# Who copies the second half of the turned probabilities out of PSUM: ScalarE before, VectorE after

## The chip, the cores and the metric

The kernel runs on one core of one Trainium2 chip. The time is the device time of one execution in microseconds; of the kernel before, three runs took 2648.97, 2649.49 and 2653.16 us, median 2649.49.

## The reference, cut to what matters

The input `x` is 128 sequences of 64 tokens with 256 features. The network has two blocks: a transformer block with modulation (attention and MLP), and a second block with attention over 16 heads of 64 features, with normalised queries and keys, followed by eight experts that each pick their tokens. The change lies in the attention of the second block:

```
h = _ln(x, ln1_g, ln1_b) + shift
qkv = (h @ Wqkv.T).reshape(b, n, 3, H, HD)
q = _ln(qkv[:, :, 0].transpose(0, 2, 1, 3), qn_g, qn_b)
k = _ln(qkv[:, :, 1].transpose(0, 2, 1, 3), kn_g, kn_b)
v = qkv[:, :, 2].transpose(0, 2, 1, 3)
scores = jnp.einsum('bhnd,bhmd->bhnm', q, k) / jnp.sqrt(jnp.float32(HD))
attn = jax.nn.softmax(scores, axis=-1)
o = jnp.einsum('bhnm,bhmd->bhnd', attn, v)
x = x + o.transpose(0, 2, 1, 3).reshape(b, n, H * HD) @ Wout.T
```

## The kernel before, in words

The phases run one after the other with a barrier between them: setup, first attention, MLP, second attention (`attention1_phase`, lines 847 to 1196), routing, experts. In the second attention a step `i` handles one tile of 128 tokens, which is two sequences of 64. There are NT = 64 tiles. Each engine has its own instruction stream, written out by hand, with semaphores between the streams; a step of any stream holds work for several tiles at once: `has(0)` guards the work on tile `i` (queries, keys, values), `has(-1)` that on tile `i-1` (softmax, product with the values, output projection), `has(-2)` the end of tile `i-2` (residual, gate scores, store) and `has(1)` the layer norm of tile `i+1`. An engine takes its instructions strictly in the order of its stream, so a wait holds up all that stands behind it.

The part of a step in which the change lies, stream by stream:

- TensorE (from line 1086): scores of tile `i-1` (L1097), products for queries and keys (lines 115 to 117 through `split_product`) and values, gate scores (L1147), the probabilities of tile `i-1` turned in two groups of four transposes, the first into `b_b[0]`, the second into `b_b[1]` (L1157, semaphores `pT0` and `pT1`), `turn_qk(0, 1)` (four transposes, L1111), the wait for the copied probabilities (L1164), the product of probabilities and values (L1173, 64 small matmuls), `turn_qk(1, QG)` (12 transposes, each group of four behind `qkn`), and the output projection, whose first half waits for the first `o_lo` and whose second half waits for the second. `turn_next` (L1118) turns `xhat` of the next tile between the halves.
- ScalarE (from line 903): squares of queries and keys (L919) with the exponentials (L906) after the first, `values_out(0)` (L911), gate scores (L929), the two copies of the turned probabilities from PSUM into `PT` (L934), `values_out(1)`, the high parts `o_hi` (L941), `qT` and `kT` (L944, L946).
- VectorE (from line 972): `hT`, `h_hi`, `h_lo` (L997 to L1007), residual, row maximum and shift of the scores, sums and moments of the squares (L975, L991), sum and scale of the probabilities (L1045 to L1053), `sums(2)`, `moments(2)`, `scaled(0)`, `sums(3)`, `moments(3)`, then `xhat` (L1066), `scaled(1)`, `scaled(2)`, `scaled(3)` (L983, query and key groups read from PSUM and multiplied by the inverse root), and the two `o_lo` (L1075).
- GpSimd: the inverse roots (L961, L966), one per group, each behind its `moments`.

Two PSUM tensors of one bank each, `b_b[0]` and `b_b[1]`, serve in turn the transposed probabilities, the output of L1173, the projection and the turned `xhat`.

Of the kernel before, what the change touches and what calls it, by code (L numbers as in the profile page):

```python
# [90 lines left out]
def pipeline_by(by, eng, step, n, before, after):  # L91


    def edge(i):
        step(i, lambda k: 0 <= i + k < n, i % by)
    first = after + -after % by
    last = n - before - (n - before - first) % by
    for i in range(-before, first):
        edge(i)
    with eng.Fori(0, (last - first) // by) as turn:  # L100
        for phase in range(by):
            step(by * turn + first + phase, lambda k: True, phase)
    for i in range(last, n + after):
        edge(i)


def later(t):

    return not isinstance(t, int) or t > 0
# [737 lines left out]
def attention1_phase(nc, a, out, g):  # L847

    with ExitStack() as ctx:
# [19 lines left out]
        PT = m.sb("a1_PT", [P, H // 2, P])  # L869
        o_hi, o_lo = (m.sb("a1_o_" + n, [P, V1], F32R) for n in ("hi", "lo"))  # L870
        xs = m.sb("a1_xs", [P, D])
        xsT = m.sb("a1_xsT", [P, DC, P])
# [3 lines left out]
        BK = 512  # L876
        b_b = [m.ps(f"a1_bb{n}", BK) for n in range(2)]
        names = ("stats aggr eps rstd xhat xT hT h_hi h_lo qk sq red vq rq qkn qkT q_out k_out v v_out s maxed "
                 "shifted exped summed recip probs pT0 pT1 pT_out o o_hi o_lo proj res xsT xsT_out lg lg_out "
                 "stored wout wv_in wv_hi wv_lo wout_hi wout_lo pe_held").split()  # L880
        s = {n: m.sem("a1_" + n) for n in names}
        ident = g.cst[:, C_ID:C_ID + P]
# [5 lines left out]
        with nc.Block() as block:  # L888
            @block.sync
            def _(sp):  # L890
                def store(t):
                    sp.wait_ge(s["res"], t + 1)
                    sp.dma_start(g.tok_dram[t][:, 0:D], xs[:, :]).then_inc(s["stored"], 16)
                    sp.dma_start(out[t], xs[:, :]).then_inc(s["stored"], 16)
                sp.dma_start(wv, a["qkv1_w"][:, :, QK1:]).then_inc(s["wv_in"], 16)
                sp.dma_start(wout[:, :, :], a["out1_w"]).then_inc(s["wout"], 16)
                with sp.Fori(0, NT) as t:
                    store(t)
                sp.wait_ge(s["stored"], 32 * NT)

            @block.scalar
            def _(act):
                def step(i, has, turn):
                    def exps():
                        act.wait_ge(s["shifted"], i)
                        nc.scalar.activation(pr[:, :, :], pr[:, :, :], ACT.Exp, scale=SCALE1).then_inc(s["exped"], 1)  # L906

                    def values_out(n):
                        act.wait_ge(s["v"], 2 * i + n + 1)
                        for b in range(2):  # L910
                            nc.scalar.copy(vs[n * S:(n + 1) * S, turn % 2, b, :],  # L911
                                           b_a[b * S:(b + 1) * S, n * BK:(n + 1) * BK]).then_inc(s["v_out"], 1)

                    if has(0):
                        for n in range(QG):
                            act.wait_ge(s["qk"], QG * i + n + 1)
                            if later(i):
                                act.wait_ge(s["red"], QG * i + n - QG + 1)
                            nc.scalar.activation(sq[:, n * BK:(n + 1) * BK], b_qk[:, n * BK:(n + 1) * BK],  # L919
                                                 ACT.Square).then_inc(s["sq"], 1)  # L920
                            if n == 0 and has(-1):
                                exps()
                    elif has(-1):
                        exps()
                    if has(0):
                        values_out(0)
                    if has(-2):
                        act.wait_ge(s["lg"], i - 1)
                        nc.scalar.copy(g.lg[:, :, bass.ds(i - 2, 1)], b_b[1][:, 0:E].unsqueeze(2))\  # L929
                            .then_inc(s["lg_out"], 1)  # L930
                    if has(-1):
                        for n in range(2):
                            act.wait_ge(s[f"pT{n}"], i)
                            nc.scalar.copy(PT[:, 4 * n:4 * n + 4, :].rearrange("p j q -> p (j q)"), b_b[n][:, :])\  # L934
                                .then_inc(s["pT_out"], 1)
                    if has(0):
                        values_out(1)
                    if has(-1):
                        act.wait_ge(s["o"], i)
                        for n in range(2):  # L940
                            nc.scalar.copy(o_hi[:, n * BK:(n + 1) * BK], b_b[n][:, :]).then_inc(s["o_hi"], 1)  # L941
                    if has(0):
                        act.wait_ge(s["qkT"], i + 1)
                        nc.scalar.activation(qT[:, :, :].rearrange("p j t -> p (j t)"), b_qk[:, 0:V1], ACT.Identity,  # L944
                                             bias=g.qn[:, 1:2], scale=g.qn[:, 0:1]).then_inc(s["q_out"], 1)
                        nc.scalar.activation(kT[:, :, :].rearrange("p j t -> p (j t)"), b_qk[:, V1:QK1], ACT.Identity,  # L946
                                             bias=g.kn[:, 1:2], scale=g.kn[:, 0:1]).then_inc(s["k_out"], 1)
                    if has(0) and not later(i):
                        act.wait_ge(s["wout"], 16)
                        nc.scalar.copy(wout_hi, wout[:, :, :]).then_inc(s["wout_hi"], 1)  # L950
                act.wait_ge(s["wv_in"], 16)
                nc.scalar.copy(g.wv_hi, wv).then_inc(s["wv_hi"], 1)
                act.wait_ge(g.loaded1, 16 * 3)
                pipeline_by(2, act, step, NT, 0, 3)

            @block.gpsimd
# [14 lines left out]
            def _(dve):  # L971
                def step(i, has):
                    def sums(n):
                        dve.wait_ge(s["sq"], QG * i + n + 1)
                        nc.vector.reduce_sum(ss[:, n * 8:(n + 1) * 8],  # L975
                                             sq[:, n * BK:(n + 1) * BK].rearrange("p (h d) -> p h d", d=HD1), AX)\
                            .then_inc(s["red"], 1)
# [11 lines left out]
                    def moments(n):  # L989
                        dve.wait_ge(s["red"], QG * i + n + 1)  # L990
                        nc.vector.tensor_scalar(vq[:, 8 * n:8 * n + 8], ss[:, 8 * n:8 * n + 8], 1.0 / HD1, EPS1,  # L991
                                                ALU.mult, ALU.add).then_inc(s["vq"], 1)
# [63 lines left out]
                    if has(0):  # L1056
                        sums(2)
                        moments(2)
                        scaled(0)
                        sums(3)  # L1060
                        moments(3)
                    if has(1):
                        dve.wait_ge(s["rstd"], i + 2)
                        if later(i + 1):
                            dve.wait_ge(s["xT"], i + 1)
                        nc.vector.tensor_scalar(xhat[:, :], g.X[:, i + 1, :], mv[:, 0:1], rstd[:, 0:1],  # L1066
                                                ALU.subtract, ALU.mult).then_inc(s["xhat"], 1)
# [17 lines left out]
            def _(pe):  # L1085
                def step(i, has, turn):
# [63 lines left out]
                    if has(-1):  # L1150
                        pe.wait_ge(s["probs"], i)
                        for n in range(2):
                            if n == 1 and has(-2):
                                pe.wait_ge(s["lg_out"], i - 1)
                            for k in range(4):
                                j = 4 * n + k
# [4 lines left out]
                    if has(0):  # L1161
                        turn_qk(0, 1)
                    if has(-1):
                        pe.wait_ge(s["pT_out"], 2 * i)  # L1164
                        pe.sem_inc(s["pe_held"], 1)
                        for mm in range(4):
                            for b in range(2):
                                toks = slice(b * S, (b + 1) * S)
                                for c in range(2):
                                    for r in range(2):  # L1170
                                        keys = slice(r * S, (r + 1) * S)
                                        j = 2 * mm + c
                                        last = nc.tensor.matmul(  # L1173
                                            b_b[r][c * HD1:(c + 1) * HD1, mm * P + b * S:mm * P + (b + 1) * S],
                                            vs[keys, (turn - 1) % 2, b, j * HD1:(j + 1) * HD1], PT[keys, j, toks],
                                            start=True, stop=True)
                        last.then_inc(s["o"], 1)
# [704 lines left out]
```

## Time and profile before

| | |
|---|---|
| median of three runs | 2649.49 us |
| profiled execution, device time | 2653.02 us |
| its span, first to last instruction | 2651.1 us |
| mean granted TensorE clock over the span | 0.958 |
| PE busy over the span | 2433.6 us (92%) |
| PE weight loads busy | 2108.6 us (80%) |
| DVE (VectorE) busy | 1966.7 us (74%) |
| ACT (ScalarE) busy | 1527.5 us (58%) |
| POOL (GpSimd) busy | 1037.3 us (39%) |

The names in the profile are PE for TensorE's matmuls and transposes, PEld for its weight loads, DVE for VectorE, ACT for ScalarE and POOL for GpSimd. A busy time is the sum of an engine's instruction times; consecutive instructions of one engine may overlap a little. L12 is line 12 of the kernel before; where a helper issues the matmul (lines 115 to 117) the tile names tell which product it is. The second attention lies between about 985 and 2130 us of the span.

### The profile page before, as it was taken

The page shows a single profiled execution, that of the slowest core. Times are in us where ns is not written, and L with a number is a line of the kernel's source. Part 1 is how long each engine was busy: PE and PEld are TensorE (multiplying, and loading weights), DVE is VectorE, ACT ScalarE, POOL GpSimd, SP SyncE. Part 2 cuts the span into 40 slices and gives each one's busy share as a digit, 9 for nine tenths or more (in the row PEclk, how much of TensorE's full clock was granted, in tenths as well). Part 3 has the DMA queues.
Part 4 walks back from the last instruction along what each step waited for, and adds up shares of the span by engine and source line. Part 5 has one row for each costly group of instructions (what it writes and reads, how often), then busy time and mean ns, then how long its engine had stood idle before and what let it go on. Part 6 is the DMA issues. An engine that isn't in the chain of part 4 may idle for free. (4 is left out here: it accounts for less than half of the span.)

```text
span 2651.1 us, 68410 instructions
## 1 busy us (share of the span) xinstructions
PE 2433.6 (92%) x25692; PEld 2108.6 (80%) x25692; DVE 1966.7 (74%) x3788; ACT 1527.5 (58%) x2847; POOL 1037.3 (39%) x876
## 2 busy tenths in 40 slices
PE   5999999969999989999999999999999824999997
PEld 4777777749999968888888888888888713899996
DVE  4888888856666658888888888888888768666663
ACT  2777777746666645555555655565556503555653
POOL 1676777730000013344333443344334302355544
PEclk8999999969999989999999999999999956999998
DMA  4011111010110110000000000000000021243332
GB/s 121 30 32 36 32 32 36 28 25 23 30 30 20 29 50 13 16 12 16 16 16 13 14 16 16 16 12 16 16 16 12 17 56 41 80 91 91 78 71 32
DMA packets 86352, 89.19 MB, mean 34 GB/s; under 512 B 26753, under 2 KB 80641, under 8 KB 83585
## 3 DMA queue, kind: packets, MB, share of 16 engines
q1 hardware_dynamic: 73984, 71.08, 8.9%
q0 software_dynamic: 12288, 17.05, 4.0%
q8 instruction: 51, 0.84, 0.1%
q14 instruction: 29, 0.23, 0.0%
HBM read 62.40 MB, written 25.69 MB: 33 GB/s over the span
## 5 line engine op out<-in xcount | busy, mean ns | idle before, releaser
L966 POOL TENSOR_TENSOR a_rq<-a_vq,minus_half 128x8 f32<-128x8 f32 x256 | 417.3, 1651 | 104.2 <-DVE a_vq L991 104.2
L919 ACT ACTIVATE a_sq<-a_bqk 128x512 f32<-128x512 f32 x256 | 152.0, 594 | 318.1 <-PE a_bqk L117 318.1
L961 POOL TENSOR_TENSOR a_rstd<-a_veps,minus_half 128x1 f32<-128x1 f32 x64 | 35.3, 552 | 628.4 <-DVE a_veps L1035 628.4
L115 PE MATMUL a_bqk<-wqk_hi,a_h_lo 128*128 128x512 f32 x512 | 207.3, 405 | 5.1 <-DVE a_h_lo L1007 5.1
L117 PE MATMUL a_bqk<-wqk_hi,a_h_hi 128*128 128x512 f32 x512 | 201.7, 394 | 0.0
L116 PE MATMUL a_bqk<-wqk_lo,a_h_hi 128*128 128x512 f32 x512 | 201.3, 393 | 0.0
L983 DVE TENSOR_TENSOR a_qk<-a_bqk,a_rq 128x512 f32<-128x512 f32 x256 | 170.6, 687 | 28.8 <-POOL a_rq L966 28.8
L1663 DVE TENSOR_TENSOR e_u_lo<-e_u,e_u_hi 128x512 fp32r<-128x512 f32 x128 | 88.8, 693 | 127.3 <-ACT e_u_hi L1526 123.2
L431 POOL TENSOR_TENSOR a_kbd<-a_kT,consts_sb 128x512 f32<-128x512 f32 x128 | 130.9, 1044 | 125.7 <-PE a_bs L556 122.5
L911 ACT COPY a_vs<-a_ba 64x512 f32<-64x512 f32 x256 | 149.0, 582 | 53.6 <-PE a_ba L117 48.9
L1521 ACT ACTIVATE e_u<-e_bu,e_b 128x512 f32<-128x512 f32 x128 | 88.3, 690 | 156.6 <-PE e_bu L117 152.7
L975 DVE TENSOR_REDUCE a_ss<-a_sq 128x8 f32<-128x512 f32 x256 | 173.2, 677 | 1.4 <-ACT a_sq L919 1.4
L680 ACT ACTIVATE m_u<-m_bu,m_b 128x512 f32<-128x512 f32 x128 | 88.4, 691 | 130.2 <-PE m_bu L117 130.2
L115 PE MATMUL a_bb<-w_parts,a_o_lo 128*128 128x256 f32 x512 | 155.9, 304 | 1.5 <-DVE a_o_lo L1075 1.4
L773 DVE TENSOR_TENSOR m_u_lo<-m_u,m_u_hi 128x512 fp32r<-128x512 f32 x128 | 88.3, 690 | 91.5 <-ACT m_u_hi L687 89.4
L698 POOL TENSOR_TENSOR m_rstd<-m_veps,minus_half 128x4 f32<-128x4 f32 x16 | 21.7, 1355 | 322.4 <-DVE m_veps L714 322.4
L123 PE MATMUL e_by<-e_w_hi,e_u_lo 128*128 128x256 f32 x512 | 145.4, 284 | 0.0
L123 PE MATMUL m_by<-w_parts,m_u_lo 128*128 128x256 f32 x512 | 145.2, 284 | 0.0
L125 PE MATMUL e_by<-e_w_hi,e_u_hi 128*128 128x256 f32 x512 | 144.8, 283 | 0.0
L124 PE MATMUL e_by<-e_w_lo,e_u_hi 128*128 128x256 f32 x512 | 144.8, 283 | 0.0
L116 PE MATMUL a_bb<-w_parts,a_o_hi 128*128 128x256 f32 x512 | 143.9, 281 | 0.0
L117 PE MATMUL a_bb<-w_parts,a_o_hi 128*128 128x256 f32 x512 | 143.8, 281 | 0.0
(244 smaller groups left out, 7828.6 us busy)
## 6 DMA issues: line engine op xcount, KB each, us to landing
X<-in_x SPq DMA_DIRECT2D x64, 128.0 KB
a_gate<-gates_of_rows SPq DMA_DIRECT2D x128, 64.0 KB, 2.5
m_gate<-gates_of_rows SPq DMA_DIRECT2D x32, 256.0 KB, 4.3
tokens<-a_xs SPq DMA_DIRECT2D x64, 128.0 KB, 1.7
out<-a_xs SPq DMA_DIRECT2D x64, 128.0 KB, 1.7
e_w<-in_fc1s SPq DMA_DIRECT2D x8, 1024.0 KB, 4.7
e_w<-in_fc2s SPq DMA_DIRECT2D x8, 1024.0 KB, 4.8
a_w<-in_fc_w SPq DMA_DIRECT2D x2, 1024.0 KB, 6.2
```

The lines of the kernel that those rows point to most:

```text
L115: tensor.matmul(to, w_lo, x_hi, start=start, stop=False)
L116: tensor.matmul(to, w_hi, x_lo, start=False, stop=False)
L117: return tensor.matmul(to, w_hi, x_hi, start=False, stop=stop)
L123: tensor.matmul(to, w_lo, x_hi, start=start, stop=False, skip_group_check=True)
L124: tensor.matmul(to, w_hi, x_lo, start=False, stop=False, skip_group_check=True)
L125: return tensor.matmul(to, w_hi, x_hi, start=False, stop=stop, skip_group_check=True)
L431: last = nc.gpsimd.tensor_tensor(kbd[:, c, :, :], kT[:, c, :].unsqueeze(1).to_broadcast([P, 4, P]), g.cst[:, C_QUAD:C_QUAD + 4].unsqueeze( ...
L911: nc.scalar.copy(vs[n * S:(n + 1) * S, turn % 2, b, :], b_a[b * S:(b + 1) * S, n * BK:(n + 1) * BK]).then_inc(s["v_out"], 1)
L919: nc.scalar.activation(sq[:, n * BK:(n + 1) * BK], b_qk[:, n * BK:(n + 1) * BK], ACT.Square).then_inc(s["sq"], 1)
L966: nc.gpsimd.tensor_tensor(rq[:, 8 * n:8 * n + 8], vq[:, 8 * n:8 * n + 8], g.mhalf[:, 0:8], ALU.pow).then_inc(s["rq"], 1)
L975: nc.vector.reduce_sum(ss[:, n * 8:(n + 1) * 8], sq[:, n * BK:(n + 1) * BK].rearrange("p (h d) -> p h d", d=HD1), AX)\
L983: nc.vector.tensor_tensor(qk[:, n * BK:(n + 1) * BK].rearrange("p (h d) -> p h d", d=HD1), b_qk[:, n * BK:(n + 1) * BK].rearrange("p (h d) ...
```

## The change

ScalarE's loop over both halves becomes a copy of the first half alone. VectorE gets the second half, between `moments(3)` and `xhat`, behind a wait for `pT1`, and counts it in a semaphore of its own. TensorE waits for both counts. The data, the buffers and the order of everything else stay.

```diff
@@ scalar
                     if has(-1):
-                        for n in range(2):
-                            act.wait_ge(s[f"pT{n}"], i)
-                            nc.scalar.copy(PT[:, 4 * n:4 * n + 4, :].rearrange("p j q -> p (j q)"), b_b[n][:, :])\
-                                .then_inc(s["pT_out"], 1)
+                        act.wait_ge(s["pT0"], i)
+                        nc.scalar.copy(PT[:, 0:4, :].rearrange("p j q -> p (j q)"), b_b[0][:, :])\
+                            .then_inc(s["pT_out"], 1)
@@ vector
                         scaled(0)
                         sums(3)
                         moments(3)
+                    if has(-1):
+                        dve.wait_ge(s["pT1"], i)
+                        nc.vector.tensor_copy(PT[:, 4:8, :].rearrange("p j q -> p (j q)"), b_b[1][:, :])\
+                            .then_inc(s["pT_out_v"], 1)
                     if has(1):
                         dve.wait_ge(s["rstd"], i + 2)
@@ tensor
                     if has(-1):
-                        pe.wait_ge(s["pT_out"], 2 * i)
+                        pe.wait_ge(s["pT_out"], i)
+                        pe.wait_ge(s["pT_out_v"], i)
                         pe.sem_inc(s["pe_held"], 1)
```

## Rows read from the trace of the kernel before

**Rows 1.** Stretches of one step each (start:end, length, busy time and count per engine).
```profile
core 0: us, PE busy (x) PEld busy (x) DVE busy (x) ACT busy (x) POOL busy (x), PEclk, DMA share, GB/s
1500.00:1517.64 17.64, 17.31 (x222) 15.12 (x221) 14.66 (x30) 10.33 (x17) 7.08 (x5) 1.00 0.04 15
...
sum 141.12, PE 138.48 PEld 120.84 DVE 117.39 ACT 82.70 POOL 56.60; mean PE 17.31 PEld 15.11 DVE 14.67 ACT 10.34 POOL 7.07
```

**Rows 2.** Waits from 1008 to 2110 us (total us, times, longest).
```profile
DVE a_hT L997 <- PE a_bb L1118: 91.6, 62, 1.5
...
DVE a_o_lo L1075 <- ACT a_o_hi L941: 30.4, 62, 0.6
DVE a_qk L983 <- POOL a_rq L966: 27.6, 63, 0.8
...
PE a_bb L1173 <- ACT a_PT L934: 20.9, 63, 0.4
...
PEld a_bb L115 <- DVE a_o_lo L1075: 12.4, 62, 0.2
...
DVE a_xs L1014 <- issue: 7.4, 41, 0.2
```

**Rows 3.** Instructions of one step in order of time (start, length, idle before).
```profile
1518.80 1.16 PE L1157 MATMUL a_bb<-consts_sb,a_p 128*128 128x128 f32 x8
...
1519.25 0.17 DVE L991 TENSOR_SCALAR a_vq<-a_ss 128x8 f32<-128x8 f32 x1
1519.33 0.41 DVE L1066 TENSOR_SCALAR a_xhat<-X,a_mv,a_rstd 128x256 f32 x1
1519.47 1.11 ACT L934 COPY a_PT<-a_bb 128x512 f32<-128x512 f32 x2 [0.23 <-PE a_bb L1157]
1519.66 1.28 DVE L983 TENSOR_TENSOR a_qk<-a_bqk,a_rq 128x512 f32<-128x512 f32 x2
...
1520.69 1.05 PEld L1173 LDWEIGHTS a_bb<-a_PT,a_vs 64*64 64x64 f32 x64 [0.54 <-issue]
1520.72 1.16 PE L1173 MATMUL a_bb<-a_PT,a_vs 64*64 64x64 f32 x64 [0.33 <-ACT a_PT L934]
1521.38 0.69 DVE L983 TENSOR_TENSOR a_qk<-a_bqk,a_rq 128x512 f32<-128x512 f32 x1 [0.43 <-POOL a_rq L966]
...
1521.81 1.53 PE L1111 MATMUL a_bqk<-consts_sb,a_qk 128*128 128x128 f32 x12
1521.94 1.08 ACT L941 CAST a_o_hi<-a_bb 128x512 fp32r<-128x512 f32 x2 [0.15 <-PE a_bb L1173]
1522.56 1.29 DVE L1075 TENSOR_TENSOR a_o_lo<-a_bb,a_o_hi 128x512 fp32r<-128x512 f32 x2 [0.49 <-ACT a_o_hi L941]
1523.30 0.19 PEld L115 LDWEIGHTS a_bb<-w_parts,a_o_lo 128*128 128x128 f32 x1 [0.20 <-DVE a_o_lo L1075]
...
1523.38 1.21 ACT L944 ACTIVATE a_qT<-a_bqk,qn 128x1024 f32<-128x1024 f32 x1 [0.37 <-PE a_bqk L1111]
...
1524.49 1.20 ACT L946 ACTIVATE a_kT<-a_bqk,kn 128x1024 f32<-128x1024 f32 x1
...
1524.77 0.38 PE L1118 MATMUL a_bb<-consts_sb,a_xhat 128*128 128x128 f32 x2
...
1525.31 0.61 DVE L997 SCALAR_TENSOR_TENSOR a_hT<-a_bb,ln1g,shift 128x128 f32<-128x128 f32 x2 [1.46 <-PE a_bb L1118]
...
1526.28 0.42 DVE L1007 TENSOR_TENSOR a_h_lo<-a_hT,a_h_hi 128x256 fp32r<-128x256 f32 x1
...
1526.46 1.16 PE L1097 MATMUL a_ba<-a_kT,a_qT 64*64 64x64 f32 x64
```

**Rows 4.** All instructions of line 934 (min/median/max ns, first and last start).
```profile
L934 ACT COPY a_PT<-a_bb x128: 586/586/591, 1008.2 to 2117.6; 128x512 f32<-128x512 f32 x128
```

**Rows 5.** Groups from 1026 to 2096 us (busy us, mean ns, idle before).
```profile
L934 ACT COPY a_PT<-a_bb 128x512 f32<-128x512 f32 x122 | 67.0, 586 | 14.4 <-PE a_bb L1157 14.4
...
L1041 DVE COPY a_xsT<-a_bb 128x256 f32<-128x256 f32 x61 | 25.5, 418 | 0.0
...
L1005 DVE CAST a_h_hi<-a_hT 128x256 fp32r<-128x256 f32 x61 | 18.0, 294 | 2.1
```

More of the change, by code:

```diff
@@ L878, in attention1_phase @@
         names = ("stats aggr eps rstd xhat xT hT h_hi h_lo qk sq red vq rq qkn qkT q_out k_out v v_out s maxed "
-                 "shifted exped summed recip probs pT0 pT1 pT_out o o_hi o_lo proj res xsT xsT_out lg lg_out "
+                 "shifted exped summed recip probs pT0 pT1 pT_out pT_out_v o o_hi o_lo proj res xsT xsT_out lg lg_out "
                  "stored wout wv_in wv_hi wv_lo wout_hi wout_lo pe_held").split()
```

## The prediction

> **What bounds the kernel now.** I read the page first for the three engines' shares, then the stretches of the second attention, then its waits, then one step in order of time. The change touches only that phase. Its loop makes 64 steps; ScalarE's first copy of the turned probabilities starts at 1008.2 us and its last at 2117.6 [rows 4], which over 63 intervals is 17.61 us a step. TensorE's matmuls cover 17.31 us of a 17.64 us step at a granted clock of 1.00, VectorE's work 14.67 and ScalarE's 10.34 [rows 1]. So TensorE's order sets the period: a step gets longer by what TensorE is made to stand in it, and by nothing else. It stands twice now. It waits for ScalarE's copies before the product with the values (PE L1173, 20.9 us in 63 steps, 0.33 each), and for VectorE's low part before the output projection (the weight load of L115 behind `o_lo`, 12.4 us in 62, 0.20 each) [rows 2]. Between these two waits lies everything that the change moves.
>
> In one step [rows 3] the reader should see this. The eight transposes of the probabilities run from 1518.80 to 1519.96. ScalarE copies both halves back to back, 1519.47 to 1520.58, so the second half is copied while VectorE is already further on: at 1519.42 it has finished `moments(3)` (L991), and it goes straight on to `xhat` (1519.33, started before the former had drained), `scaled(1)` and `scaled(2)` (1519.66), waits 0.43 for GpSimd's root, does `scaled(3)` (1521.38), waits 0.49 for ScalarE's `o_hi` and starts `o_lo` at 1522.56. TensorE loads its first value tile at 1520.69, 0.11 behind the copy's end, and the first projection weight at 1523.30, 0.05 behind the end of the first `o_lo` (1522.56 + 0.69).
>
> **The change, part by part.** *Removed from ScalarE*: one 128x512 copy of 0.586 us a step [rows 5]. What follows it there is `values_out(1)`, then the wait for `o`. The values are wanted only by the next step's products and `o_hi` waits for TensorE, so ScalarE's saved time is worth nothing: it already stands for 0.15 us before `o_hi` [rows 3].
>
> *Added to VectorE*: a wait for the second four transposes and a copy, placed ahead of `xhat` and `scaled(1..3)`. The wait is real. Those transposes end at 1519.96; VectorE is free at 1519.42. It restarts 0.16 behind a transpose (L1118 ends at 1524.77 + 0.38 = 1525.15, L997 starts at 1525.31) [rows 3], so the copy starts at 1520.12 and the engine loses 0.70 us. For the copy's length the trace has no 128x512 copy on VectorE. Below it stands the 128x256 copy out of PSUM, 0.418 us, above it the 128x512 PSUM reads of L983 at 0.69 [rows 3, 5]; 256 columns more cost 0.27, so I take 0.68. It ends at 1520.80.
>
> *The first half of the effect, at the values.* The probabilities were complete at 1520.58 and will be at 1520.80. TensorE's load follows 0.11 later if the gap seen behind ScalarE's copy holds (there is a semaphore increment between wait and load there), 0.05 if the gap behind `o_lo` does: 1520.91 or 1520.85, that is 0.22 or 0.16 later than 1520.69. The two waits instead of one on TensorE's queue I cost at nothing: ScalarE's count is met half a microsecond before.
>
> *The second half, which I expect to decide.* VectorE's next instruction starts 0.09 before the former's end (L991 to L1066). So `xhat` starts at 1520.71 instead of 1519.33; `scaled(1)` 0.33 later at 1521.04, then 0.60 each: `scaled(2)` 1521.64, `scaled(3)` 1522.24. GpSimd's root is long there, so that 0.43 us of waiting disappears. The first `o_lo` can start 0.60 after `scaled(3)`, at 1522.84. Its other input, `o_hi`, comes with TensorE's delay: 1522.56 + 0.22 = 1522.78. VectorE's own queue is the later by 0.06, and `o_lo` starts 0.28 later than before. In other words 1.38 us are put in front of the chain, 0.43 + 0.49 of old waits swallow 0.92, and 0.46 less the two overlaps with neighbours (0.60 of pitch against 0.69 of length, twice) is what remains.
>
> *TensorE behind it.* After the values (1.09 us) it turns 12 query and key tiles from 1522.03 on, 0.11 apart. The last four need `scaled(3)`, done at 1522.93 and seen at 1522.98; TensorE would reach them at 1522.91, so this costs 0.07 inside the shadow of `o_lo` and it is through at 1523.42. The projection needs `o_lo` at 1522.84 + 0.69 + 0.05 = 1523.58: 0.28 behind 1523.30. After that nothing gives it back. ScalarE's `qT` and `kT` start 0.29 later and end at 1525.98, while the next scores start at 1526.46 + 0.28; cover 0.76. VectorE's 1.46 us wait before `hT` [rows 2, 3] comes after `o_lo`, ends with TensorE's own transposes and so moves along; the low part `h_lo` ends at 1526.70, before the scores end at 1527.62. The slack VectorE has is thus in the wrong place.
>
> *Sum.* 63 steps have both this copy and a following query/key tile: 63 x 0.28 = 17.6 us. The 64th has no `scaled` work behind it and pays only the later copy, 0.2. Together 17.8 us. The profiled execution took 2653.0 us (span 2651.1) and would take 2670.8; against the median of 2649.5, from which I predict, 2667.3.
>
> **Bounds.** Lowest: restart after 0.06 us, as ScalarE does behind L1173, and a copy as short as ScalarE's 0.586. The copy ends at 1520.61, `o_lo` starts at 1522.65, +0.09 a step, 6 us: 2655. Highest: VectorE, having stood at the wait, also stalls once for issue as it does before L1014 (7.4 us in 41 times, 0.18 each [rows 2]): +0.46 a step, 29 us: 2679. I take the middle value because each term has a row of the same engine and nearly the same form.
>
> **Rivals.** *The moved work disappears among waits: no change.* VectorE would go from 14.67 to 15.35 us of 17.6, still under TensorE's 17.31, with 1.5 us of waiting before `hT`. For it: 0.92 us of old waits really is swallowed. Against it: the queue is in order and the copy's own wait of 0.70 us must be paid as well as its 0.68. It would need restart plus copy within 0.56 us where I have 0.84. Time 2649.5, chance 8%.
> The Trainium skill ("Perfetto Trace Analysis", section Identifying the Most-Contended Engine) says that one improves a kernel by improving its most-contended engine; by that rule moving a copy between two engines that both have room beside TensorE would leave the time as it is. The trace agrees that both have room, but the order in which VectorE's room comes speaks against the conclusion.
>
> *The copy runs at the rate of VectorE's SBUF casts: faster.* The cast of 128x256 from SBUF takes 0.294 us against 0.418 for the copy from PSUM [rows 5]. At the cast's rate 512 columns take about 0.43; with a restart of 0.06 the copy ends at 1520.45, before ScalarE's two copies end now, `o_lo` starts at 1522.50, 0.06 sooner, and the time is 2649.5 - 3.8 = 2645.7. It decides from a restart plus copy under 0.56 us. Against it: the only copy out of PSUM in the trace is at the slower rate, and the restart would have to be far below the 0.16 us read behind L1118. Chance 3%.
> The Trainium skill ("VectorE: DVE Perf Modes", section The perf-mode tier table) allows a copy with a PSUM operand up to twice the plain rate, and the paragraph behind it says that fp32 from PSUM gets the plain rate only; this trace agrees with the second, by the 0.418 and 0.294 us above. At twice the rate, and with the 120 fixed cycles that the same page's section The TRN2 errata gives for PSUM reads, the copy would last an estimated 0.39 us and the time would not change; no run here shows that.
>
> *Reading PSUM beside ScalarE and TensorE slows the copy, or the issue stall above appears.* For: for the first time both engines read the probability banks in one stretch. Against: L983 reads PSUM during ScalarE's copies now and keeps its 0.69. From +0.40 a step on: 2675 to 2680, chance 6%.
>
> *The change doesn't act*, because ScalarE's queue or another chain set the wait: excluded by the 0.11 us between copy and load. No chance of its own.
>
> **From cases to numbers.** The forecast (+0.09 to +0.40 a step) has 83%, the rivals 8, 3 and 6. A measurement of this kernel tells about 0.2%, 5.3 us or 0.08 us a step, from no change. Faster by more: 3%, wanting both ends of the fast case and some luck. Within it: the hidden case, most of the fast one and the forecast's low corner, 9%. Slower: 88%. The range reaches from 2655, the low bound, to 2677, near the high one.
>
> **What would show it.** Right, if in a step of the changed kernel VectorE waits about 0.7 us for PE L1157 and then copies for 0.68; if its wait for GpSimd's root before `scaled(3)` and its wait for `o_hi` are both near zero; if TensorE's wait at L1173 grows from 0.33 to about 0.5 and the load's wait for `o_lo` grows from 0.20 to about 0.3; and if the step is 17.90 us. Wrong in the second half, if VectorE still waits for `o_hi`: then the values' delay alone decides (+0.16 to +0.22, 2660 to 2663). Wrong altogether, if the granted clock of the stage leaves 1.00, since every term is a duration at that clock.

## The result and the profile after

The changed kernel takes 2661.21 us in the median against 2650.56 of the kernel before on the same chip; the ratio is 1.0036 with a 95% interval of 1.0024 to 1.0049, so 6.4 to 13.0 us slower, 9.5 in the middle. One of the seven executions of the changed kernel took 3492.35 us at a mean granted clock of 0.646, against 0.958 to 0.963 in the other six, and does not enter the ratio; the median of those six is 2660.92 us. The forecast of 17.8 us slower had the sign and the place right and was almost twice too large. The profiled execution took 2660.62 us (span 2658.8), 7.6 more than the profiled one of before.

All of that lies in the second attention's loop. Its length can be read in one row, the scores' matmuls of all steps with the start of the first and of the last. Of the kernel after:

```profile
L1100 PE MATMUL a_ba<-a_kT,a_qT x4096: 218/218/366, 991.8 to 2116.7; 64*64 64x64 f32 x196
```

That is 1124.9 us. The same row of the kernel before (its L1097) runs from 991.9 to 2108.9, 1117.0 us. The difference, 7.9 us, is 0.125 us for each of 63 steps, where the forecast had 0.28; the stretches ahead of the loop and behind it differ by no more than 0.1 us. "The loop" means this length from here on.

Eight steps of the kernel after (stretch, length, busy time and count per engine), which answer to [rows 1]:

```profile
1500.00:1517.75 17.75, 17.36 (x221) 15.05 (x220) 15.18 (x31) 9.82 (x16) 7.09 (x6) 1.00 0.04 15
...
sum 142.00, PE 138.85 PEld 120.38 DVE 121.33 ACT 78.41 POOL 56.56; mean PE 17.36 PEld 15.05 DVE 15.17 ACT 9.80 POOL 7.07
```

The granted clock is still 1.00. VectorE works 0.50 us more a step and ScalarE 0.54 less. VectorE's rise is less than the 0.69 of the copy, because two instructions that used to start after a wait (`scaled(3)` and the first `o_lo`) now overlap their neighbours by 0.09 each.

Waits of the kernel after, 1008 to 2118 us, which answer to [rows 2]:

```profile
DVE a_hT L996 <- PE a_bb L1121: 91.1, 62, 1.5
...
ACT a_o_hi L940 <- PE a_bb L1177: 46.2, 63, 0.9
...
DVE a_PT L1063 <- PE a_bb L1160: 35.7, 62, 0.6
...
PE a_bb L1177 <- issue: 23.6, 60, 0.4
...
PEld a_bb L115 <- DVE a_o_lo L1078: 11.1, 62, 0.2
...
DVE a_xs L1013 <- issue: 0.9, 5, 0.2
```

VectorE's two old waits in this chain, for GpSimd's root before `scaled(3)` and for `o_hi` before `o_lo`, are gone from the list. A new one of 0.58 us a step stands in front of the copy. ScalarE gained nothing: the 0.15 us that it stood before `o_hi` became 0.73. TensorE's wait before the values has grown from 0.33 to 0.39 and is now put down to "issue". The 1.5 us before `hT` are as long as ever. The wait of the projection's weight load for `o_lo` did not grow: 0.18 us a step instead of 0.20.

One step of the kernel after (start, length, idle before), to set beside [rows 3]:

```profile
1504.70 1.14 PE L1160 MATMUL a_bb<-consts_sb,a_p 128*128 128x128 f32 x8
...
1505.15 0.17 DVE L990 TENSOR_SCALAR a_vq<-a_ss 128x8 f32<-128x8 f32 x1
1505.37 0.58 ACT L933 COPY a_PT<-a_bb 128x512 f32<-128x512 f32 x1 [0.24 <-PE a_bb L1160]
...
1505.87 0.69 DVE L1063 COPY a_PT<-a_bb 128x512 f32<-128x512 f32 x1 [0.55 <-PE a_bb L1160]
...
1506.48 0.40 DVE L1069 TENSOR_SCALAR a_xhat<-X,a_mv,a_rstd 128x256 f32 x1
1506.63 1.05 PEld L1177 LDWEIGHTS a_bb<-a_PT,a_vs 64*64 64x64 f32 x64 [0.60 <-issue]
...
1506.80 1.88 DVE L982 TENSOR_TENSOR a_qk<-a_bqk,a_rq 128x512 f32<-128x512 f32 x3
...
1507.76 1.64 PE L1114 MATMUL a_bqk<-consts_sb,a_qk 128*128 128x128 f32 x12
1507.88 1.07 ACT L940 CAST a_o_hi<-a_bb 128x512 fp32r<-128x512 f32 x2 [0.72 <-PE a_bb L1177]
1508.60 1.28 DVE L1078 TENSOR_TENSOR a_o_lo<-a_bb,a_o_hi 128x512 fp32r<-128x512 f32 x2
1509.33 0.19 PEld L115 LDWEIGHTS a_bb<-w_parts,a_o_lo 128*128 128x128 f32 x1 [0.18 <-DVE a_o_lo L1078]
...
1510.82 0.38 PE L1121 MATMUL a_bb<-consts_sb,a_xhat 128*128 128x128 f32 x2
1511.35 0.61 DVE L996 SCALAR_TENSOR_TENSOR a_hT<-a_bb,ln1g,shift 128x128 f32<-128x128 f32 x2 [1.47 <-PE a_bb L1121]
```

Count from the end of the eight transposes (1504.70 + 1.14 = 1505.84). The copy starts 0.03 behind it, the values' first load comes 0.79 behind it (0.73 before), the first `o_lo` 2.76 behind it (2.60 before). `o_lo` starts with no idle time before it, straight from `scaled(3)`: VectorE's own queue decides, and `o_hi` had been there since 1507.88 + 0.59 = 1508.47. The projection's first load follows the end of the first `o_lo` as before, and is 0.15 us later (3.49 behind the transposes, 3.34 before). TensorE stands for that in three places: 0.06 more before the values, 0.11 more in the twelve transposes, whose last four wait for `scaled(3)` (1.64 us for the twelve, 1.53 before), and 0.02 less before the projection.

The second half was already copied at once before the change: ScalarE's second copy started at 1519.47 + 1.11 - 0.59 = 1519.99 [rows 3], 0.03 behind the transposes, as VectorE's does now. The whole delay of the probabilities is the longer copy, 0.69 against 0.59 us.

The copy's own row, over all steps:

```profile
L1063 DVE COPY a_PT<-a_bb x64: 683/692/693, 1008.7 to 2125.4; 128x512 f32<-128x512 f32 x64
```

### The profile page after: what moved, and what is told of

Same layout as the page of the kernel before. It is cut to its first block and busy times, and to the rows that moved or that the text cites. A ratio compares the mean times of both kernels' runs of the same rounds, so it can differ in the third digit from the quotient of the medians.

```text
span 2658.8 us, 68351 instructions
## 1 busy us (share of the span) xinstructions
PE 2434.1 (92%) x25691; PEld 2103.5 (79%) x25692; DVE 1999.3 (75%) x3852; ACT 1492.8 (56%) x2783; POOL 1035.9 (39%) x876
## 5 line engine op out<-in xcount | busy, mean ns | idle before, releaser
L982 DVE TENSOR_TENSOR a_qk<-a_bqk,a_rq 128x512 f32<-128x512 f32 x256 | 164.9, 685 | 1.3 <-POOL a_rq L965 1.3
L1114 PE MATMUL a_bqk<-consts_sb,a_qk 128*128 128x128 f32 x1024 | 143.0, 279 | 1.0 <-DVE a_qk L982 0.9
L124 PE MATMUL m_by<-w_parts,m_u_hi 128*128 128x256 f32 x512 | 143.8, 281 | 0.0
```

Of the source, the lines that this page charges most:

```text
L124: tensor.matmul(to, w_hi, x_lo, start=False, stop=False, skip_group_check=True)
L982: nc.vector.tensor_tensor(qk[:, n * BK:(n + 1) * BK].rearrange("p (h d) -> p h d", d=HD1), b_qk[:, n * BK:(n + 1) * BK].rearrange("p (h d) ...
L1114: last = nc.tensor.transpose(b_qk[:, j * P:(j + 1) * P], qk[:, j * P:(j + 1) * P], ident)
```

## The experiments

Theory A is the forecast's mechanism: the projection's first weight load follows `o_lo`, and `o_lo` starts at the later of two things, VectorE's queue up to it and `o_hi` behind the values. Theory B says that only the second counts: the probabilities are complete later, so the values are. Theory C says that a copy on VectorE costs by itself, by its work, its PSUM reads or its semaphore. All kernels ran beside the kernel before on their chip.

| kernel | loop us | per step against before | median us | ratio, 95% interval |
|---|---|---|---|---|
| before | 1117.0 | | 2650.56 | |
| after | 1124.9 | +0.125 | 2661.21 | 1.0036, 1.0024 to 1.0049 |
| xhat ahead of the copy | 1121.1 | +0.065 | 2656.12 | 1.0017, 1.0007 to 1.0026 |
| halves exchanged | 1117.0 | 0.000 | 2651.14 | 1.0002, 0.9993 to 1.0011 |
| wait without copy | 1117.0 | 0.000 | 2651.66 | 1.0002, 0.9993 to 1.0011 |
| one more copy | 1147.2 | +0.479 | 2681.80 | 1.0117, 1.0102 to 1.0133 |
| copy behind scaled(1) | 1137.5 | +0.325 | 2673.25 | 1.0082, 1.0069 to 1.0096 |
| restart | 1129.7 | +0.202 | 2664.90 | 1.0052, 1.0036 to 1.0067 |
| transposes early | 1094.7 | -0.354 | 2629.61 | 0.9915, 0.9901 to 0.9928 |
| transposes early, with the change | 1094.9 | -0.351 | 2629.32 | 0.9918, 0.9904 to 0.9931 |

The kernel before ran at 2651.05 us beside the first four experiments and at 2652.75 beside the last four.

### The wait without the copy

An edit of the kernel before, in VectorE's stream:

```diff
                         moments(3)
+                    if has(-1):
+                        dve.wait_ge(s["pT1"], i)
                     if has(1):
```

> The kernel before, both copies on ScalarE, with nothing added but VectorE's wait for the second four transposes ahead of xhat. Theory A: the wait costs VectorE 0.57 us, which its old waits of 0.43 and 0.49 us before scaled(3) and o_lo swallow; step 17.63, kernel 2650 us. A rival to it (a wait in VectorE's queue delays xhat or a scaled group that TensorE is waiting for): over 17.70 us a step, over 2655 us.

Measured: no difference in the loop. VectorE's standing has only moved forward; the wait for `o_hi` shrank and the one for the root all but vanished (waits of this kernel):

```profile
DVE a_xhat L1068 <- PE a_bb L1159: 34.6, 61, 0.6
...
DVE a_o_lo L1077 <- ACT a_o_hi L941: 21.9, 61, 0.4
...
DVE a_qk L983 <- POOL a_rq L966: 0.4, 1, 0.4
```

That is 0.57 us a step in the new wait and 0.36 in the one for `o_hi`, 0.93 together, where [rows 2] have 0.44 for the root and 0.49 for `o_hi`. The new wait alone is free.

### One more copy on VectorE

An edit of the kernel after, in VectorE's stream:

```diff
                             .then_inc(s["pT_out_v"], 1)
+                        nc.vector.tensor_copy(spare[:, :], pr[:, 0:8, :].rearrange("p h k -> p (h k)"))
```

> The changed kernel with one more VectorE copy, of 128x512 from SBUF to a spare tile, right behind the new copy, behind its semaphore, so that the probabilities are complete no later. It computes nothing that is used. Theory A: the chain up to o_lo has no slack left, so nearly the whole of the extra 0.35 to 0.43 us appears in the step: 18.07 to 18.17 us, kernel 2682 to 2688 us. Theory B: the step stays at 17.75 and the kernel at 2661 us.

The spare copy, from SBUF, takes 0.42 us (VectorE's copy of the same size from PSUM takes 0.69) and moves `xhat` by 0.33. The median, 2681.80 us, lies 0.2 below the range that A had given. The loop grows by 22.3 us over that of the kernel after, 0.354 a step, although the probabilities are complete at the same moment. B is out as the whole story. The step in order of time shows TensorE waiting for each of the three `scaled` groups, before the old wait at the projection:

```profile
1499.55 0.42 DVE L1066 COPY a_spare<-a_p 128x512 f32<-128x512 f32 x1
...
1500.20 1.88 DVE L983 TENSOR_TENSOR a_qk<-a_bqk,a_rq 128x512 f32<-128x512 f32 x3
1500.94 0.42 PEld L1116 LDWEIGHTS a_bqk<-consts_sb,a_qk 128*128 128x128 f32 x4 [0.18 <-DVE a_qk L983]
...
1501.54 0.42 PEld L1116 LDWEIGHTS a_bqk<-consts_sb,a_qk 128*128 128x128 f32 x4 [0.18 <-DVE a_qk L983]
...
1502.13 0.42 PEld L1116 LDWEIGHTS a_bqk<-consts_sb,a_qk 128*128 128x128 f32 x4 [0.18 <-DVE a_qk L983]
```

### xhat ahead of the copy

An edit of the kernel after, in VectorE's stream:

```diff
-                    if has(-1):
-                        dve.wait_ge(s["pT1"], i)
-                        nc.vector.tensor_copy(PT[:, 4:8, :].rearrange("p j q -> p (j q)"), b_b[1][:, :])\
-                            .then_inc(s["pT_out_v"], 1)
                     if has(1):
                         dve.wait_ge(s["rstd"], i + 2)
...
                                                 ALU.subtract, ALU.mult).then_inc(s["xhat"], 1)
+                    if has(-1):
+                        dve.wait_ge(s["pT1"], i)
+                        nc.vector.tensor_copy(PT[:, 4:8, :].rearrange("p j q -> p (j q)"), b_b[1][:, :])\
+                            .then_inc(s["pT_out_v"], 1)
                     if has(0):
```

> The changed kernel with VectorE's new copy moved behind xhat, so that xhat runs in the time in which VectorE otherwise stands for the transposes. In the changed kernel the copy starts 0.04 us behind the last transpose and lasts 0.69, and the first o_lo starts 0.16 us later than before. Theory A (VectorE's queue up to o_lo decides, its chain is one xhat of 0.33 us shorter here): o_lo then waits for o_hi again, which is only 0.065 us later than before, so the step is 17.67 to 17.70 us and the kernel 2653 to 2655 us. Theory B (the later end of the copy, and with it the values' delay, decides): the copy ends where it does in the changed kernel, so the step stays at 17.75 and the kernel at 2661 us.

Measured: `xhat` runs inside the wait, the copy starts when it did, and half of the loss is gone, 0.065 us a step left. One step, from the transposes on:

```profile
1502.29 1.14 PE L1160 MATMUL a_bb<-consts_sb,a_p 128*128 128x128 f32 x8
...
1502.81 0.41 DVE L1065 TENSOR_SCALAR a_xhat<-X,a_mv,a_rstd 128x256 f32 x1
...
1503.47 0.69 DVE L1069 COPY a_PT<-a_bb 128x512 f32<-128x512 f32 x1 [0.24 <-PE a_bb L1160]
...
1504.23 1.05 PEld L1177 LDWEIGHTS a_bb<-a_PT,a_vs 64*64 64x64 f32 x64 [0.60 <-issue]
...
1506.10 1.29 DVE L1078 TENSOR_TENSOR a_o_lo<-a_bb,a_o_hi 128x512 fp32r<-128x512 f32 x2
```

The values' load comes 0.80 behind the transposes as in the kernel after, `o_lo` 2.67 behind them instead of 2.76. What remains is B's part: the probabilities are complete 0.11 us later, VectorE's copy being 0.69 long where ScalarE's is 0.59, and the values' load comes 0.06 later. The median came out one microsecond above what A had given; the ratio, +4.5 us, agrees with the loop's +4.1.

### The halves exchanged

An edit of the kernel after, in ScalarE's and VectorE's streams:

```diff
-                        act.wait_ge(s["pT0"], i)
-                        nc.scalar.copy(PT[:, 0:4, :].rearrange("p j q -> p (j q)"), b_b[0][:, :])\
+                        act.wait_ge(s["pT1"], i)
+                        nc.scalar.copy(PT[:, 4:8, :].rearrange("p j q -> p (j q)"), b_b[1][:, :])\
...
-                        dve.wait_ge(s["pT1"], i)
-                        nc.vector.tensor_copy(PT[:, 4:8, :].rearrange("p j q -> p (j q)"), b_b[1][:, :])\
+                        dve.wait_ge(s["pT0"], i)
+                        nc.vector.tensor_copy(PT[:, 0:4, :].rearrange("p j q -> p (j q)"), b_b[0][:, :])\
```

> The changed kernel with the halves exchanged: VectorE copies the first half, ScalarE the second, both at the same places in their queues. VectorE's copy can start 0.5 us sooner. Theory A: the chain up to o_lo ends before o_hi is there, the copies end when they did before the change; step 17.63, kernel 2650 us, no gain although both copies overlap, since the second cannot start before its transposes. Theory B: the same, since the last copy ends as before. Theory C (one copy more on VectorE costs by itself, by its work, its PSUM reads or its semaphore): 17.70 to 17.75 us a step and 2655 to 2661 us.

Measured: the loop of the kernel before, to the tenth of a microsecond. VectorE makes the same number of copies of the same size, so C is out. Its copy starts 0.04 us behind the end of the first four transposes, and VectorE hardly stands for it; ScalarE waits for the other four:

```profile
1500.25 0.69 DVE L1063 COPY a_PT<-a_bb 128x512 f32<-128x512 f32 x1
1500.75 0.59 ACT L933 COPY a_PT<-a_bb 128x512 f32<-128x512 f32 x1 [0.75 <-PE a_bb L1160]
...
1501.45 1.05 PEld L1177 LDWEIGHTS a_bb<-a_PT,a_vs 64*64 64x64 f32 x64 [0.54 <-issue]
...
1503.32 1.29 DVE L1078 TENSOR_TENSOR a_o_lo<-a_bb,a_o_hi 128x512 fp32r<-128x512 f32 x2 [0.26 <-ACT a_o_hi L940]
```

The two copies do overlap, by 0.19 us, and nothing is won: the second half is copied from the moment its transposes end, as before. Whichever engine copies it, it cannot start sooner. Copying the second half in two parts, one on each engine, was not tried.

### The copy behind scaled(1)

An edit of the kernel with `xhat` ahead of the copy, in VectorE's stream:

```diff
+                    if has(0):
+                        scaled(1)
                     if has(-1):
                         dve.wait_ge(s["pT1"], i)
...
                     if has(0):
-                        for n in range(1, QG):
+                        for n in range(2, QG):
                             scaled(n)
```

> The changed kernel with VectorE's copy moved further back, behind xhat and scaled(1). The copy then starts when scaled(1) drains, 0.27 us later than in the changed kernel, and the probabilities are complete 0.38 us later than before the change. VectorE's chain up to o_lo is shorter than in the changed kernel, so the other input of o_lo, o_hi behind the values, should now be the later one. Theory A (o_lo starts at the later of VectorE's queue and o_hi): o_lo 0.33 us later than before, step 17.92 to 17.95, kernel 2669 to 2672 us. A theory by which VectorE's queue alone counts would have the step at 17.63 to 17.70 and the kernel at 2650 to 2655 us.

Measured: 0.325 us a step, with `o_lo` 0.33 later than before as A had it; the median, 2673.25 us, is 1.3 above A's range. Here `o_hi` is the later input again, and VectorE stands for it:

```profile
1507.93 1.14 PE L1162 MATMUL a_bb<-consts_sb,a_p 128*128 128x128 f32 x8
...
1509.38 0.68 DVE L1071 COPY a_PT<-a_bb 128x512 f32<-128x512 f32 x1
...
1510.13 1.05 PEld L1179 LDWEIGHTS a_bb<-a_PT,a_vs 64*64 64x64 f32 x64 [0.86 <-issue]
...
1512.00 1.29 DVE L1080 TENSOR_TENSOR a_o_lo<-a_bb,a_o_hi 128x512 fp32r<-128x512 f32 x2 [0.74 <-ACT a_o_hi L940]
```

With the kernel after this shows both arms of theory A: the queue decides there, `o_hi` here. In all three places tried, ahead of `xhat`, behind it and behind `scaled(1)`, VectorE's copy of the second half loses.

### The restart behind a wait

An edit of the kernel after, in VectorE's stream:

```diff
+                        dve.wait_ge(s["pT0"], i)
                         dve.wait_ge(s["pT1"], i)
...
-                                g.sh_1[:, c, bass.ds(2 * i, 2)].unsqueeze(2).to_broadcast([P, 2, S]),
+                                g.sh_1[:, c, 0:2].unsqueeze(2).to_broadcast([P, 2, S]),
```

> Why VectorE's copy starts 0.04 us behind the last transpose, where hT starts 0.15 behind a transpose of the same shape. The changed kernel with two alterations: a second wait in front of the copy, for the first four transposes, long met; and hT reads the shift of sequences 0 and 1 at a fixed address instead of one computed from the loop's counter, so that the shift of the other sequences is left out. If a second wait costs, the copy starts 0.1 us behind the transpose and the step is 0.05 to 0.1 longer than 17.75. If the computed address costs, hT starts 0.04 to 0.06 behind its transpose instead of 0.15, with no effect on the step, since TensorE does not wait for hT. If neither, both stay as they are and the time is 2661 us.

Measured: both cost.

```profile
1503.84 1.14 PE L1161 MATMUL a_bb<-consts_sb,a_p 128*128 128x128 f32 x8
...
1505.09 0.69 DVE L1064 COPY a_PT<-a_bb 128x512 f32<-128x512 f32 x1 [0.64 <-PE a_bb L1161]
...
1510.04 0.38 PE L1122 MATMUL a_bb<-consts_sb,a_xhat 128*128 128x128 f32 x2
...
1510.45 0.61 DVE L996 SCALAR_TENSOR_TENSOR a_hT<-a_bb,ln1g,shift 128x128 f32<-128x128 f32 x2 [1.36 <-PE a_bb L1122]
```

The copy starts 0.11 behind the transposes (1504.98 to 1505.09) where it was 0.03 with one wait: the second wait, long met, costs 0.08. `hT` starts 0.03 behind its transposes (1510.42 to 1510.45) where it was 0.15 in the kernel after (1511.20 to 1511.35): the address computed from the loop's counter costs 0.12. Over all steps the medians give 0.07 for the wait and 0.11 for the address. The loop grows by 4.8 us over that of the kernel after, 0.076 a step, which is the second wait once more: in the kernel after every delay of the copy reaches the end.

### The transposes early

An edit of the kernel before. TensorE's stream first, then ScalarE's, where `values_out(n, first, end)` copies the sequences `first` to `end - 1` alone:

```diff
                         values(0)
-                        values(1)
                     if has(-2):
                         pe.wait_ge(s["xsT_out"], i - 1)
...
                             last.then_inc(s[f"pT{n}"], 1)
+                    if has(0):
+                        values(1)
                     if has(0):
                         turn_qk(0, 1)
...
-                    if has(0):
-                        values_out(0)
                     if has(-2):
                         act.wait_ge(s["lg"], i - 1)
...
                     if has(0):
-                        values_out(1)
+                        values_out(0)
+                        values_out(1, 0, 1)
                     if has(-1):
                         act.wait_ge(s["o"], i)
...
                     if has(0):
+                        values_out(1, 1, 2)
                         act.wait_ge(s["qkT"], i + 1)
```

> The kernel before, both copies on ScalarE, with TensorE's order changed: gate scores and the eight transposes of the probabilities stand between values(0) and values(1) instead of behind both. ScalarE's order follows: gate scores and the two copies first, then values_out(0), half of values_out(1), o_hi, the other half. If the copies are bounded by when the transposes end, as the run with exchanged halves suggests, then they end about 1 us before TensorE asks for them, its 0.5 us of standing before the product with the values goes, and the first o_lo starts about 0.4 us sooner, bounded by o_hi and scaled(3) together: step 17.20 to 17.30 us, kernel 2624 to 2630 us. A rival: GpSimd's last root, or ScalarE, which now has 1.8 us of value copies ahead of o_hi, takes the place of the wait; then 17.4 us or more and 2636 us or more.

Measured: 0.354 us a step less and 0.85% faster than the kernel before (interval 0.72 to 0.99%). The probabilities are complete at 1508.61, TensorE loads its first value tile at 1509.73:

```profile
1506.83 1.15 PE L1156 MATMUL a_bb<-consts_sb,a_p 128*128 128x128 f32 x8
...
1507.50 1.11 ACT L932 COPY a_PT<-a_bb 128x512 f32<-128x512 f32 x2 [0.23 <-PE a_bb L1156]
...
1509.73 1.02 PEld L1174 LDWEIGHTS a_bb<-a_PT,a_vs 64*64 64x64 f32 x64 [0.17 <-issue]
...
1510.74 0.69 DVE L983 TENSOR_TENSOR a_qk<-a_bqk,a_rq 128x512 f32<-128x512 f32 x1 [0.43 <-POOL a_rq L966]
...
1510.96 1.07 ACT L940 CAST a_o_hi<-a_bb 128x512 fp32r<-128x512 f32 x2 [0.67 <-PE a_bb L1174]
1511.58 1.29 DVE L1075 TENSOR_TENSOR a_o_lo<-a_bb,a_o_hi 128x512 fp32r<-128x512 f32 x2
```

TensorE's matmuls have no wait before the values any more. The rivals of the expectation did not come: GpSimd's last root is waited for as before (27.5 us in the whole loop, 27.6 in [rows 2]), and ScalarE is through with its value copies 0.67 us before `o` is there. `o_lo` now starts 0.03 behind `o_hi` and 0.15 behind `scaled(3)`; its two inputs come almost together. VectorE's queue would let `o_lo` start 0.60 behind `scaled(3)`, at 1511.34 instead of 1511.58, so an earlier `o_hi` could bring 0.24 us a step at most (an estimate from these rows) and a shorter queue nothing.

### The transposes early, with the change

The kernel above with the diff under study applied to it.

> The order of TensorE and ScalarE as in the run with the early transposes, and in it the change under study: VectorE copies the second half, at the same place, between moments(3) and xhat. The transposes are then done before VectorE is, so it does not stand at the wait, and the values do not need the copy at once. Theory A: VectorE's chain gets 0.6 us longer and takes up its old waits; the step is within 0.05 us of the same order with both copies on ScalarE, 17.20 to 17.30, 2624 to 2632 us. Theory C (the second engine's copy costs by itself): 0.1 us a step or more, 6 us, slower than that order with both copies on ScalarE.

Measured: the same loop to 0.2 us. The copy starts with no wait when VectorE reaches it, and the values do not want it for another 0.35 us:

```profile
1507.34 0.68 DVE L1063 COPY a_PT<-a_bb 128x512 f32<-128x512 f32 x1
...
1508.38 1.02 PEld L1178 LDWEIGHTS a_bb<-a_PT,a_vs 64*64 64x64 f32 x64 [0.17 <-issue]
```

The same edit that costs 0.125 us a step in the one order costs nothing in the other.

## Why the prediction was right, and where it was too large

**The place and the sign.** Everything outside the loop stayed, the clock stayed at 1.00, VectorE's old waits swallowed most of the added work, the rest came out at `o_lo`. The forecast said that the queue, not `o_hi`, decides there; the row without idle time before L1078 shows it, and "one more copy" and "the copy behind scaled(1)" show the two arms apart. Shown by experiment.

**The term that was mis-sized is VectorE's restart.** I took 0.16 us, from `hT` behind L1118 in [rows 3], because it was the same engine behind a transpose of the same shape. It is 0.03. The row I read was of an instruction with an address computed from the loop's counter, the copy has none; the restart run shows the 0.12 between them. A nearer row stood in [rows 3]: ScalarE's second copy, behind the very transposes in question, starts 0.03 behind them. Put 0.03 in place of 0.16 into the forecast's own chain and `o_lo` comes 0.15 us later instead of 0.28; measured 2.76 - 2.60 = 0.16. My lower bound had used 0.06, from ScalarE behind L1173; it would have been the better choice.

**The copy's length**, 0.68 forecast, is 0.692. The pitches behind it (0.60 per group, 0.33 for `xhat`) held: from copy to `o_lo` 2.73 us in the trace (1505.87 to 1508.60), 2.72 in the forecast.

**The values' delay**, forecast as 0.16 or 0.22, is 0.06, by the same restart. With 0.69 + 0.03 the copy ends 0.72 behind the transposes and the load follows 0.07 later, so here the gap of 0.05 that I had read behind `o_lo` fits better than the 0.11 behind ScalarE's copy. TensorE's wait before the values grew to 0.39, not to about 0.5.

**A sign that did not follow from the forecast.** The load's wait for `o_lo` was to grow from 0.20 to about 0.3. By the forecast's own chain TensorE is through with its transposes at 1523.42 and loads at 1523.58, 0.16 apart; the same count for the kernel before, 1521.81 + 12 x 0.11 = 1523.13 to 1523.30, gives 0.17. The chain thus had no growth there, and the trace shows none (0.18): part of the standing moves ahead, to the values and to the last four transposes.

**The last 0.03.** `o_lo` is 0.16 us later, the step only 0.125 longer. Between the projection's first load and the next scores the kernel after is on average that much quicker, and nearly all of it is gained in the projection's second half, where its matmuls start 0.115 us apart instead of 0.117. Why they do is not shown and stays open.

**The rivals.** Work hidden among waits was wrong for this place, but by less than I gave it: restart plus copy came to 0.72 us, with 0.56 as the point from which it would have been hidden. The fast copy is excluded by 0.692 us for 512 columns; the spare copy from SBUF, 0.42, does run at the rate that this rival had assumed (0.43). Contention for PSUM as the cause of the loss is excluded by the exchanged halves, where both engines read the two banks together for 0.19 us, keep their 0.69 and 0.59 and lose nothing.
The Trainium skill ("VectorE: DVE Perf Modes", section Why PSUM operands drop a tier) gives fp32 from PSUM the plain rate; the 0.692 us against 0.418 for 256 columns, 1.07 ns a column, agree, and the spare copy of 512 columns from SBUF, 0.418 us, was the faster one. The table ahead of it allows up to twice the plain rate for a copy from PSUM; this fp32 copy does not reach that.
The rule of the most-contended engine (the Trainium skill, "Perfetto Trace Analysis", section Identifying the Most-Contended Engine), read as the prediction read it, would have had no change. The runs disagree where the copy's place in the queue was bad (0.125, 0.065 and 0.325 us a step) and agree in the two kernels where it was good (0.000 and 0.003).

## What to carry to other kernels

Moving work to an engine with room is judged at the instruction that TensorE waits for next: add up that engine's queue from the insertion point to it, with the wait in front of the inserted instruction, and compare it with the other input's arrival; idle time behind that point was worth nothing here. Before splitting a copy over two engines, look at what its last part waits for. Here that was a transpose, and ordering the transposes earlier was worth 23 us, where giving one of the two halves to VectorE was worth nothing at best.

## What the runs showed of the hardware that I had not expected

- VectorE's copy starts 0.03 to 0.04 us behind the modelled end of the transpose that it waits for (kernel after). A second wait in front of it, already met, adds 0.07 to 0.08; in `hT`, an address computed from the loop's counter adds 0.11 to 0.12 (restart run, against the kernel after).
- ScalarE and VectorE copying from two PSUM tensors at once, for 0.19 us, keep their lengths, 0.59 and 0.69 us (exchanged halves).
- VectorE copies 128x512 fp32 from SBUF in 0.42 us and from PSUM in 0.69 (one more copy).
